# The inverse sum of a softmax applied while the probabilities are split, not in a pass of its own

## The reference

```python
x = x + xattn(layernorm(x), ctx)
x = x + ffn(layernorm(x))

def xattn(up, down):                  # per batch, channels C = 128
    q, k, v = Wq @ up, Wk @ down, Wv @ down
    attention = softmax(q.T @ k / sqrt(C), axis=-1)      # 1024 x 256
    return Wskip @ up + v @ attention.T

def ffn(x):
    w = (nibbles(qweight) - round(zeros / scales).T) * scales.T   # 1024 x 1024
    return x @ w + bias
```

## Time and profile before

| | us |
|---|---|
| timed runs | 519.47, 520.64, 523.09; median 520.64 |
| the profiled execution | 521.43 |
| its span, first to last instruction | 519.4 |
| busy PE / DVE / ACT / POOL in the span | 497.4 / 436.5 / 378.1 / 469.3 |
| granted PE clock, mean over the span | 0.993 |

### The profile page before, as it was taken

One profiled execution on the slowest core, in us unless ns is written; L12 is line 12 of the kernel. 1 busy time (PEld: TensorE's weight loads), 2 busy tenths in 40 slices (PEclk: granted clock), 3 DMA queues, 4 the chain that ended last, 5 costly groups with the idle time before them and its releaser, 6 DMA issues.

```text
span 519.4 us, 9388 instructions
## 1 busy us (share of the span) xinstructions
PE 497.4 (96%) x2682; PEld 301.1 (58%) x2682; DVE 436.5 (84%) x1003; ACT 378.1 (73%) x868; POOL 469.3 (90%) x713
## 2 busy tenths in 40 slices
PE   4797799999999999999999999999999999999987
PEld 3453565656666565666656566665656666565644
DVE  5888998889888888988888898888889888887752
ACT  4888677777877777787777777777777877777520
POOL 4676999999999999999999999999999999999762
PEclk9899899999999999999999999999999999999999
DMA  8674577777787777787768977976787797757653
GB/s 311 195 145 124 130 169 174 195 196 185 177 205 175 179 183 192 189 181 194 184 165 190 194 184 167 195 189 180 185 196 186 173 197 183 179 130 146 165 132 116
DMA packets 227203, 92.65 MB, mean 178 GB/s; under 512 B 209488, under 2 KB 214352, under 8 KB 227152
## 3 DMA queue, kind: packets, MB, share of 16 engines
q1 hardware_dynamic: 226432, 91.91, 73.9%
q10 hardware_dynamic: 720, 0.14, 0.1%
HBM read 23.87 MB, written 16.78 MB: 78 GB/s over the span
## 4 chain that ended last, share of the span: by engine, by line
PE 84%; DVE 5%; POOL 4%; DMA 3%; issue 2%; ACT 1%; SPq 0%; POOLq 0%; ACTq 0%; DVEq 0%
PE ps_y L1022 38%; PE ps_e L976 15%; PE ps_o L1017 13%; PE ps_o L1011 7%; PE ps_kv L994 2%; PE ps_y L1028 2%; PE ps_kv L990 2%; DMA sb_xnt_lo<-sb_xn_lo 2%; PE ps_e L972 1%; POOL sb_xn_lo L318 1%; POOL sb_prob L273 1%; DMA sb_x<-in_x_dram 1%; DVE sb_st L722 1%; DVE sb_neg_max L698 1%; ACT sb_prob L506 1%
## 5 line engine op out<-in xcount | busy, mean ns | idle before, releaser
L1022 PE MATMUL ps_y<-sb_wf,sb_xnt_hi 128*128 128x512 f16 x496 | 188.3, 380 | 3.1 <-DMA sb_xnt_lo<-sb_xn_lo 2.9
L1022 PE MATMUL ps_y<-sb_wf,sb_xnt_lo 128*128 128x512 f16 x496 | 188.0, 379 | 0.0
L506 ACT ACTIVATE sb_prob<-ps_e,sb_neg_max 128x256 f32<-128x256 f32 x256 | 118.1, 470 | 52.8 <-DVE sb_neg_max L698 52.8
L273 POOL TENSOR_SCALAR sb_prob<-sb_prob,sb_rsum 128x256 f32<-128x256 f32 x256 | 122.7, 492 | 9.3 <-DVE sb_rsum L703 9.3
L707 DVE TENSOR_TENSOR sb_p_lo<-sb_prob,sb_p_hi 128x1024 f16<-128x1024 f32 x64 | 78.1, 1220 | 36.3 <-ACT sb_p_hi L515 36.3
L267 POOL TENSOR_TENSOR sb_o<-sb_prod,sb_x 128x512 f32<-128x512 f32 x63 | 84.9, 1348 | 6.2 <-DVE sb_prod L741 6.2
L698 DVE TENSOR_REDUCE sb_neg_max<-ps_e 128x2 f32<-128x512 f32 x128 | 85.2, 683 | 3.5 <-PE ps_e L972 3.2
L976 PE MATMUL ps_e<-sb_k_hi,sb_xc_hi 128*128 128x256 f32 x232 | 81.4, 351 | 3.9 <-issue 3.9
L515 ACT ACTIVATE sb_p_hi<-sb_prob 128x1024 f16<-128x1024 f32 x64 | 67.3, 1052 | 22.9 <-issue 22.5
L1022 PEld LDWEIGHTS ps_y<-sb_wf,sb_xnt_hi 128*128 128x128 f16 x496 | 48.4, 98 | 60.6 <-DMA sb_xnt_lo<-sb_xn_lo 4.3
L1022 PEld LDWEIGHTS ps_y<-sb_wf,sb_xnt_lo 128*128 128x128 f16 x496 | 48.5, 98 | 54.7
(11 more groups left out here) (150 smaller groups left out, 984.3 us busy)
## 6 DMA issues: line engine op xcount, KB each, us to landing
sb_x<-in_x_dram SPq DMA_DIRECT2D x32, 512.0 KB, 3.9
out_dram<-sb_o SPq DMA_DIRECT2D x63, 256.0 KB, 2.4
sb_ctx<-in_ctx_dram SPq DMA_DIRECT2D x32, 128.0 KB, 2.6
sb_q<-in_L_ffn_qweight_dram SPq DMA_DIRECT2D x4, 512.0 KB, 7.6
sb_pt_hi<-sb_p_hi SPq DMA_TRANSPOSE x64, 3.1
sb_pt_lo<-sb_p_lo SPq DMA_TRANSPOSE x64, 2.9
sb_scale_row<-in_L_ffn_scales_dram SPq DMA_DIRECT2D x1, 512.0 KB, 9.8
sb_xnt_hi<-sb_xn_hi SPq DMA_TRANSPOSE x32, 2.8
```

The lines of the kernel that those rows point to most:

```text
L273: last = pool.tensor_scalar(prob[:, j, t, :], prob[:, j, t, :], rsum[:, j, t:t + 1], P_SCALE, ALU.mult, ALU.mult)
L506: done = act.activation(prob[:, j, t, :], ps_e[j % 2][:, t, :], ACT.Exp, bias=neg_max[:, j, t:t + 1], accum_out=esum[:, j, t:t + 1])
L1022: pe.matmul(ps_y[h][:, :], xnt_p[s][:, q % 2, kt, :], wf[:, kt, h * HALF:(h + 1) * HALF], start=kt == 0 and s == 0, stop=False)
```

## The change

`normalise` on POOL no longer passes over the probabilities: it makes `pscale`, the inverse sums times 2 to the 14th, two columns for a chunk. `prob` stays as the exponential left it. ACT multiplies by `pscale` while it rounds, tile by tile, since the factor is one value for each of the 128 rows of a tile: four instructions of 256 columns for a half in place of one of 1024. DVE multiplies `prob` by `pscale` again and subtracts `p_hi`, also four instructions for a half. POOL gets a wait for `plo_done` of the batch before, since `pscale` is overwritten.

```diff
             def normalise(b, j):
                 pool.wait_ge(rsum_done[j], b + 1)
-                for t in range(TPC):
-                    last = pool.tensor_scalar(prob[:, j, t, :], prob[:, j, t, :], rsum[:, j, t:t + 1], P_SCALE,
-                                              ALU.mult, ALU.mult)
+                if ran(b, 1):
+                    pool.wait_ge(plo_done[j // 2], b)
+                last = pool.tensor_scalar(pscale[:, j, :], rsum[:, j, :], P_SCALE, None, ALU.mult)
                 last.then_inc(norm_done[j], 1)
...
-                act.activation(p_hi[:, h, :, :].rearrange("n k (t m) -> n k t m", m=P),
-                               prob[:, 2 * h:2 * h + 2, :, :].rearrange("n j t (k m) -> n k (j t) m", m=P),
-                               ACT.Copy).then_inc(phi_done[h], 1)
+                for j in (2 * h, 2 * h + 1):
+                    for t in range(TPC):
+                        tile = (j - 2 * h) * TPC + t
+                        last = act.activation(p_hi[:, h, :, tile * P:(tile + 1) * P],
+                                              prob[:, j, t, :].rearrange("n (k m) -> n k m", m=P),
+                                              ACT.Copy, scale=pscale[:, j, t:t + 1])
+                last.then_inc(phi_done[h], 1)
...
-                dve.tensor_tensor(p_lo[:, h, :, :].rearrange("n k (t m) -> n k t m", m=P),
-                                  prob[:, 2 * h:2 * h + 2, :, :].rearrange("n j t (k m) -> n k (j t) m", m=P),
-                                  p_hi[:, h, :, :].rearrange("n k (t m) -> n k t m", m=P),
-                                  ALU.subtract).then_inc(plo_done[h], 1)
+                for j in (2 * h, 2 * h + 1):
+                    for t in range(TPC):
+                        cols = slice(((j - 2 * h) * TPC + t) * P, ((j - 2 * h) * TPC + t + 1) * P)
+                        last = dve.scalar_tensor_tensor(p_lo[:, h, :, cols],
+                                                        prob[:, j, t, :].rearrange("n (k m) -> n k m", m=P),
+                                                        pscale[:, j, t:t + 1], p_hi[:, h, :, cols], ALU.mult, ALU.subtract)
+                last.then_inc(plo_done[h], 1)
```

More of the change, by code:

```diff
@@ L93, in xattn_ffn_program @@
         rsum = sb("rsum", [P, CHUNKS, TPC])
+        pscale = sb("pscale", [P, CHUNKS, TPC])
         p_hi, p_lo = (sb(n, [P, HALVES, MT, HALF], F16) for n in ("p_hi", "p_lo"))
```

## The result

The changed kernel takes 562.35 us (median of four runs, 561.74 to 564.1), beside 521.0 for the kernel before (four runs, 519.47 to 523.09): 1.080 times as long [1.076 to 1.084]. The forecast was slower, 531 us, within 519.5 to 545: the direction was right, the size was wrong by a factor of four.

The account below looks back on a forecast made before the run. PE was taken to set the 15.15 us period. The loop's terms summed to 15.55, 0.40 more for 28 periods: 521.43 + 11.2 + 0.6 - 1.0 = 532.2, less 0.8, said as 531 us; 8-in-10 range 519.5 to 545.

Parts of the forecast that it names:

- a loop through DVE, POOL and ACT: One trip round these engines each period: 14.92 us before, 15.55 after the change, 0.40 above PE's 15.15.
- Rival A: The loop stays hidden, 15.07 us against PE's 15.15, and only the ends count: about 520.2 us; chance 0.22.
- C: POOL gets nothing in between the four subtractions, `nb2` ends at 1.76 us: loop 16.33, about 553 us; chance 0.05.
- D: POOL was the bound and the time falls; only the ends could give, 2 us; chance 0.02.
- Rival B: POOL's `xn_lo` gets ahead of the fourth `p_lo` subtraction, costing 1.02 us each period: about 560 us; chance 0.09.
- slack behind PE: DVE's wait for PE's `ps_kv`, the loop's only slack: 0.23 us a period, taken off 15.15 to give 14.92.
- `wsk_lo` and its neighbours: DVE's `wsk_lo`, on the loop, gets shorter without POOL's normalisation reading beside it: minus 0.15 us.
- `nb2`: POOL's one-column `nb2` gets in behind the second subtraction, at 0.77, and ends at 0.98 instead of 1.34: minus 0.36 us.
- `p_hi` in four: ACT's rounding of the second half, one instruction of 1.05 us, becomes four of 1.70 together: plus 0.65 us.
- `p_lo` in four, small reads: DVE's one subtraction of 1.14 us becomes four of 1.55: plus 0.41; POOL's small reads between them: plus 0.08.
- lower bound of 0.33 a piece: Lower bound for DVE's four `p_lo` subtractions, 0.33 us each, as one input from PSUM costs something: plus 0.2.
- The ends: Outside the steady periods: plus 0.6 us in the first batch, minus 1.0 us at the kernel's end.

Follow-up runs that it names:

- e4: The kernel before with POOL's part alone: it makes `pscale`, which nothing uses, and the normalisation is left out; 520.7 us, ratio 1.000.
- e6: The changed kernel reordered: ACT rounds the second half before it normalises `xn`, POOL makes the last `pscale` before the inverse root; 524.5 us, ratio 1.008.
- e1: The changed kernel with POOL's `xn_lo` also waiting until the second half's `p_lo` is done; 537.8 us, ratio 1.033.
- e2: The kernel before with ACT's part alone: `p_hi` in four instructions with a column of ones as scale; 537.1 us, ratio 1.031.
- e3: The kernel before with DVE's part alone: `p_lo` in four fused instructions with a column of ones as scale; 527.4 us, ratio 1.013.
- e8: The changed kernel with ACT's part undone: one rounding for a half, without the scale; 524.1 us, ratio 1.006.
- e7: The kernel before with ACT's and DVE's parts together, a column of ones as scale, POOL normalising as before; 546.3 us, ratio 1.049.
- e9: The changed kernel with POOL filling an unused buffer of 256 columns just ahead of `xn_lo`; 563.0 us, ratio 1.081.
- e13: The changed kernel with POOL filling an unused buffer of 512 columns just ahead of `xn_lo`; 539.6 us, ratio 1.036.

## Why the prediction was right and wrong, by its steps

**What bounds the kernel: right.** PE sets the beat, a loop through DVE, POOL and ACT lies just below it, and POOL's share is no bound. e4 shows the last, e6 that PE is full once the loop is opened. Rival A (hidden) fell: all of e1, e2 and e3 have longer periods. Rivals C and D fell: `nb2` takes 0.70 in the median, and nothing got faster. Rival B is what happened, with the sign that was named for it, one subtraction of over 1 us in each period (1.39).

**The loop without the collision: right in sum, by errors that cancel.** e1's trip is 15.56 us, forecast 15.55. By term:

| term | forecast | measured | from |
|---|---|---|---|
| slack behind PE | -0.23 | -0.36 | row max to variance 9.27 to 8.69, less the next line's 0.26; and 0.04 ahead of the row maximum. Where DVE waited for `ps_kv`, the next instruction starts 0.59 us after the row maximum in e1, not 0.92: the wait cost 0.33, its idle time in the row is 0.24 |
| `wsk_lo` and its neighbours | -0.15 | -0.26 | what is left of that step; 0.23 of it is `wsk_lo`, which takes 0.34 us in this period of e1 and took 0.57 in that of the kernel before (by the medians, 492 to 343 ns, 0.15) |
| `nb2` | -0.36 | -0.04 | variance to `xn` 1.67 to 1.63 |
| `p_hi` in four | +0.65 | +0.64 | 1.08 to 1.72 |
| `p_lo` in four, small reads | +0.49 | +0.45 | 1.14 to 1.59 |
| sum | 15.55 | 15.56 | the forecast adds to 15.15, the measured to 15.13 |

The two prices that were taken from rows of the nearest forms came out within 0.04 us. The lower bound of 0.33 a piece, for inputs that are not from PSUM, did not: these start 0.40 us apart, where `k_lo`, with one from PSUM, had 0.39. The 0.08 for small reads had no row behind it; two of them in a group go with 1.67 us (e1), four with 1.76 (e8), so about 0.05 each (an estimate). The term of `nb2` came to nearly nothing: the step "gets in behind the second, at 0.77" failed. These are the rows of the subtraction, of `nb2` and of `wsk_lo`, after (ns min/median/max):

```profile
L715 DVE SCALAR_TENSOR_TENSOR sb_p_lo<-sb_prob,sb_pscale,sb_p_hi x256: 462/479/1401, 18.3 to 533.7; 128x256 f16<-128x256 f32 x128
L298 POOL TENSOR_SCALAR sb_nb<-sb_mv,sb_rstd x32: 264/697/723, 33.4 to 542.6; 128x1 f32<-128x1 f32 x32
L696 DVE SCALAR_TENSOR_TENSOR sb_wsk_lo<-sb_proj,sb_sk_scale,sb_wsk_hi x29: 341/343/1125, 54.8 to 510.1; 128x128 fp32r<-128x128 f32 x29
```

`nb2` starts at 300.15, +0.61 us after the first subtraction, as I had it, but ends at 300.84, +1.30: behind the third (3 x 0.39 = 1.17), not the second. In e7 it starts at +0.31 and ends at +0.91, behind the second. A one-column subtraction of POOL (L314), also wanting in at +0.61, ends at +0.93. So how long before a gap an instruction must ask is not the same for all. That `nb2` needs more lead for its two operands from memory is my guess; no run tells it.

**The step that failed, and made the size wrong,** is the sentence in rival B: "By my order of events the small ones each wait for one of the four and `xn_lo` comes behind the fourth, by 0.1 to 0.2 us." It comes ahead of the fourth by 0.19 us. I had let all four small instructions start inside the subtractions. In the kernel before the first starts ahead of the subtraction of 207.22 already (207.02), and the second only 0.07 us behind its start (207.29). And the change moves the two lists against each other. Counted from the first half's subtraction, the second half's come 4.39 us later where they came 3.79 (203.43 to 207.22; 299.54 to 303.93), mostly by the longer `p_hi`. POOL's addition ahead of the small ones waits for DVE's product behind the first half's pieces and comes 2.66 us later where it came 2.22 (205.65; 302.20). So it starts 1.73 us ahead of the subtractions, not 1.57, and two of the four small ones have begun before the first subtraction (303.54 and 303.79). My own terms held this shift, +0.65 for `p_hi` against +0.41 for `p_lo`, and I had not carried them into the order of events. The mechanism, its place and its price were on record: 1.02 us a period forecast, 0.92 measured, "about 560" against 562. What was wrong was 0.09 for its chance. An argument with a margin of 0.1 to 0.2 us, over sums each uncertain by as much, is worth about even chances, and the range should have reached to 560. That and the shift left out are faults of the working, not bad luck.

The rule that I quoted behind rival B from the Trainium skill, "SBUF — State Buffer", section "SBUF: two separate sides" (whichever starts first has the shared ports for the whole instruction), agrees with e1 and the two pauses: 1.67 us with `xn_lo` behind the fourth, 2.58 with it ahead.

The Trainium skill, "SBUF — State Buffer", section "Who interferes with whom", exempts a POOL instruction that only writes; the fills of e9 and e13 agree, 0.31 and 0.52 us in the midst of DVE's subtractions, and the group around the second keeps its 1.67.

The Trainium skill, "VectorE: DVE Perf Modes", section "The DRAIN you can't avoid", read strictly, had given four full durations. The four of 299.54 last 1.65 us in all, and the next instruction starts 1.57 after the first; each is 479 ns in the median. The exemption holds.

**The ends: too small at the start, wrong in sign at the end.** I had +0.6 and -1.0. Without the collision (e1) they are +3.3 and +2.1. Of the 6.4 us by which e1 lies above my 531.4, they are 5.8. At the start, DVE's part alone costs 1.6 and ACT's alone 1.3 (e3, e2), POOL's gives 0.6 (e4). At the end two more periods pass behind the last mark, each as much longer as the others, which accounts for 0.9 of e1's 2.1 and for 2.6 of the 4.0 after the change; the rest was not traced. I had counted one half's roundings in the first batch and a release at the end, and not that each end is a chain of several engines in which every lengthened piece counts.

## What to carry to other kernels

Where one engine is full, look for the longest closed trip through the others and its distance from the period, and ask of an edit only what it does to that trip: here 77 us of work taken off an engine that was 96% busy gained nothing (e4), and 0.65 and 0.45 us more on two others cost 17 even without the collision (e1). When a long instruction that shares memory with another engine is cut into pieces, ask what that other engine has in its list behind the short ones that used to be stuck: if it is long, it may come ahead of the last piece, and tenths of a microsecond decide that. The first remedy to try is the order of the lists: with a member taken out of the loop, the longer pieces and 1.02 us of holding cost the period nothing (e6); 0.8% stayed, most of it at the start.

## What the runs showed of the hardware that I had not expected

- POOL's small reads get in between back-to-back subtractions of DVE at almost no price to DVE: the group is 1.67 us with two of them in it (309.00 in e1) and 1.76 with four (e8).
- The same gaps let a long reader in: `xn_lo`, whose instruction takes 1.16 us, costs DVE 0.92.
- 0.22 us more pause on POOL made the kernel 23.4 us shorter (e9 to e13), though its work was longer. In e7 `xn_lo` asks at +1.28 us and is behind the fourth, so where the order turns is known only to lie between +1.14 and +1.28 us.
